# A new order of four engines' instructions in a batch loop of attention, head mixing and experts

## The reference, cut to what matters

```python
y = clip(((x * style0) @ W0.T) * demod0 + b0)          # per sample
Q, K, V = y@Wq, y@Wk, y@Wv                             # 16 heads in 4 groups, 64 wide
A = softmax(Q K^T / 8) V                               # over 128 keys
x = x + y + A @ Wpost
kx = modulated_linear(x)                               # q = k = v = kx
# per token: 16 heads of 8 features attend to one another
A2 = softmax(einsum('bnhd,bnjd->bnhj', kx, kx) / sqrt(8))
t = modulated_linear(einsum('bnhj,bnjd->bnhd', A2, kx))
x = x + experts(t)                                     # top 2 of 8 experts, capacity 640
```

## Time and profile before

| | |
|---|---|
| median of 3 runs | 538.81 us (537.04 to 538.97) |
| profiled execution | 537.42 us, its span 535.5 us |
| busy share of the span | PE 94%, PEld 67%, DVE 78%, ACT 70%, POOL 60% |
| granted TensorE clock | full in all 40 slices of the page |
| transfers | 7.19 MB in all, at the start and at the end |

### The profile page before, as it was taken

One profiled execution on the slowest core, in us unless ns is written; L12 is line 12 of the kernel. 1 busy time (PEld: TensorE's weight loads), 2 busy tenths in 40 slices (PEclk: granted clock), 3 DMA queues, 4 the chain that ended last, 5 costly groups with the idle time before them and its releaser, 6 DMA issues.

```text
span 535.5 us, 12870 instructions
## 1 busy us (share of the span) xinstructions
PE 504.0 (94%) x3896; PEld 356.4 (67%) x3896; DVE 419.3 (78%) x715; ACT 372.5 (70%) x851; POOL 323.4 (60%) x328
## 2 busy tenths in 40 slices
PE   7899999999999999999999999999999979969997
PEld 7766666666666666666666666666666756656665
DVE  4234788888888888888888888888888877754766
ACT  3467777777777777777777777777777537657783
POOL 1103677777777777777777777777777657203860
PEclk9999999999999999999999999999999999999999
DMA  6500000000000000000000000000000000000004
GB/s 228 135 1 2 2 1 2 1 0 0 0 0 0 0 0 0 0 0 0 0 0 0 0 0 0 0 0 0 0 0 1 1 2 0 2 0 2 0 11 148
DMA packets 9364, 7.19 MB, mean 13 GB/s; under 512 B 1088, under 2 KB 8832, under 8 KB 9216
## 3 DMA queue, kind: packets, MB, share of 16 engines
q1 hardware_dynamic: 9344, 6.94, 4.3%
HBM read 4.84 MB, written 2.10 MB: 13 GB/s over the span
## 4 chain that ended last, share of the span: by engine, by line
PE 52%; issue 16%; ACT 13%; DVE 12%; POOL 2%; ACTq 1%; DMA 1%; SPq 1%; DVEq 0%; POOLq 0%
PE misc L704 6%; PE bank_a L697 6%; PE bank_t L679 5%; PE bank_d L712 5%; PE bank_t L947 4%; PE bank_s L664 4%; ACT prob L1001 4%; PE bank_d L689 4%; DVE mix_lo L447 3%; DVE attT L308 3%; PE bank_t L674 2%; PE bank_s L955 2%; PE bank_d L955 2%; DVE h_den L437 2%; PE misc L834 2%
## 5 line engine op out<-in xcount | busy, mean ns | idle before, releaser
L1362 POOL TENSOR_TENSOR pair<-kx 128x1152 f32<-128x1152 f32 x32 | 82.7, 2584 | 115.2 <-DVE shifted L418 93.2
L300 DVE TENSOR_REDUCE row_max<-bank_s 128x4 bf16<-128x512 f32 x128 | 89.3, 697 | 43.0 <-PE bank_s L664 38.1
L1347 POOL TENSOR_TENSOR mix_hi<-mix_hi 128x512 f32<-128x512 f32 (+2 forms) x96 | 104.8, 1092 | 7.5
L712 PE MATMUL bank_d<-attT,wpost_sb 128*128 128x128 f32 x512 | 70.7, 282 | 1.6 <-DVE attT L308 0.6
L1001 ACT ACTIVATE prob<-bank_t 128x512 f32<-128x512 f32 x128 | 68.8, 593 | 3.6 <-PE bank_t L679 3.6
L704 PE MATMUL misc<-yT,wq_sb 128*128 128x128 f32 x512 | 68.2, 277 | 0.0
L712 PEld LDWEIGHTS bank_d<-attT,wpost_sb 128*128 128x128 f32 x512 | 62.0, 192 | 7.0 <-DVE attT L308 6.8
L679 PE MATMUL bank_t<-qT,kT 64*128 64x256 f32 x512 | 65.7, 376 | 0.0
L308 DVE TENSOR_TENSOR attT<-bank_a,inv_den 128x512 f32<-128x512 f32 x64 | 43.8, 686 | 25.1 <-ACT inv_den L1001 14.4
L704 PEld LDWEIGHTS misc<-yT,wq_sb 128*128 128x128 f32 x512 | 62.9, 194 | 0.7
L1340 POOL TENSOR_TENSOR mix_hi<-weight,kx 128x1024 f32<-128x1024 f32 x32 | 63.0, 1970 | 0.0
(11 more groups left out here) (183 smaller groups left out, 943.7 us busy)
## 6 DMA issues: line engine op xcount, KB each, us to landing
out<-acc_all SPq DMA_DIRECT2D x8, 256.0 KB, 2.3
x_all<-in_xT SPq DMA_DIRECT2D x1, 1024.0 KB, 9.8
w_sb<-in_w SPq DMA_DIRECT2D x2, 512.0 KB
x_all<-in_xT SPq DMA_DIRECT2D x1, 768.0 KB, 7.5
wq_sb<-in_wq SPq DMA_DIRECT2D x1, 512.0 KB, 6.1
wpost_sb<-in_wpost SPq DMA_DIRECT2D x1, 512.0 KB, 9.7
x_all<-in_xT SPq DMA_DIRECT2D x1, 256.0 KB, 3.2
b_rows<-in_b SPq DMA_DIRECT2D x16, 4.0 KB
```

Of the source, the lines that this page charges most:

```text
L300: V.tensor_reduce(bass.AP(row_max, first_w * (P + 1) + HPG * p, [[HPG * P, P], [P + 1, 2], [KEY, 2], [1, 1]]), bank_s[:, :, :].rearrange(" ...
L712: last = mm(bank_d[:, 0, :], wpost_sb[:, k, :], attT[:, k, :], start=(k == 0), stop=(k == CHUNKS - 1))
L1347: G.tensor_tensor(mix_hi[:, jd, 0:r, :], mix_hi[:, jd, 0:r, :], mix_hi[:, jd, r:2 * r, :], ALU.add).then_inc(s_hi, 1)
L1362: G.tensor_tensor(pair[:, :, :], bass.AP(kx2, jc * 2 * P, [[4 * P, P], [0, SHIFTS], [1, P]]), bass.AP(kx2, jc * 2 * P, [[4 * P, P], [MD, S ...
```

## The change

Within a step of the loop the helpers are called in another order on all four engines; nothing is added or removed from a step. On TensorE the fourth strip's scores come before the first half of the queries, tokens_made comes behind the first transposed scores, the y product before keys_turned and the second strip's scores, and the third strip's scores and mixing_turned stand between the halves of attend. On VectorE the sum mix_sum, the maximum h_max and shifted become separate calls, and the maxima of strips two and three move. On ScalarE six evacuations change places. On GpSimd the product for mix_hi comes first in the step, and the last two halvings behind the mirrored scores. Three fillers more stand in the first step.

```diff
@@ VectorE, loop_slot
                     if D:
                         weight_sums()
+                        weight_inverses()
                         weighted_rows()
                     if C:
                         attended()
                     head_scores()
                     if D:
                         row_sum()
+                    head_maxima()
                     if A:
                         heads_max(a, 0)
+                        heads_max(a, 1)
                     if D:
-                        weight_inverses()
-                    mixed(mix_part[:, :])
+                        rows_joined()
+                    head_shift()
+                    mixed()
                     if A:
-                        heads_max(a, 1)
-                    head_shift()
+                        heads_max(a, 2)
                     if has(a + 1):
...
                     if B:
                         normalise(s, 0)
-                    if A:
-                        heads_max(a, 2)
@@ TensorE, loop_slot
+                    if B:
+                        scores(s, j, 3)
                     if A:
                         pe.wait_ge(s_yT, n(a))
                         queries(a, 0)
-                    if B:
-                        scores(s, j, 3)
-                    if has(d - 1):
-                        tokens_made(d - 1)
...
                     if B:
                         scores_t(s, j, 0)
+                    if has(d - 1):
+                        tokens_made(d - 1)
...
                         denominators(s)
                         attend(s, j, 0)
-                        if C:
-                            pe.wait_ge(s_kx2, n(c))
-                        attend(s, j, 1)
+                    if A:
+                        scores(a, ja, 2)
                     if D:
                         if A:
                             pe.wait_ge(s_q, 2 * n(a))
                         mixing_turned(d)
-                    if A:
-                        scores(a, ja, 2)
+                    if B:
+                        if C:
+                            pe.wait_ge(s_kx2, n(c))
+                        attend(s, j, 1)
@@ ScalarE, slot
                 if A:
                     copy_q(a, ja, 0)
-                    narrow_q(a, ja, 0)
                 if B:
...
                     f(neg_diag[:, j, :, :], bank_s[:, :, :], scale=-1.0).then_inc(s_neg, 1)
-                if has(d - 1):
-                    tokens_out(d - 1)
+                if A:
+                    narrow_q(a, ja, 0)
                 if C:
                     x1_scaled()
                 if B:
                     exp_scores(s, 0)
                     exp_scores(s, 1)
+                if has(d - 1):
+                    tokens_out(d - 1)
...
+                head_weights()
                 if B:
                     invert_den(s)
-                head_weights()
```

More of the change, by code:

```diff
@@ L390, in slot, with rows_joined, mixed @@
                 ja, jc, jh, jd = 1 - j, 1 - j, j, 1 - j
-                def mixed(low):
+                def rows_joined():
+                    dve.wait_ge(s_lo, 4 * d + 4)
+                    dve.wait_ge(s_hi, 4 * d + 4)
+                    V.tensor_tensor(mix_sum[:, :], mix_part[:, :], mix_hi[:, jd, 0, :], ALU.add).then_inc(s_msum, 1)
+                def mixed():
                     if D:
-                        dve.wait_ge(s_lo, 4 * d + 4)
-                        dve.wait_ge(s_hi, 4 * d + 4)
-                        V.tensor_tensor(mix_sum[:, :], low, mix_hi[:, jd, 0, :], ALU.add).then_inc(s_msum, 1)
                         dve.wait_ge(s_hrden, n(d))
@@ L856, in loop_slot @@
                         gate_logits(parts_early[3])
+                    if has(a + 1):
+                        if A:
+                            pe.wait_ge(s_v, n(a))
+                        pe.wait_ge(s_xs, n(a + 1))
+                        mm(misc[0][:, 0, :], modw_sb[:, 0, :], xs[:, j, :], start=True, stop=True).then_inc(s_y_mm, 1)
                     if C:
@@ L861, in loop_slot @@
                     if s_is(s, -1):
-                        keep_going(3)
-                    if has(a + 1):
-                        if A:
-                            pe.wait_ge(s_v, n(a))
-                        pe.wait_ge(s_xs, n(a + 1))
-                        mm(misc[0][:, 0, :], modw_sb[:, 0, :], xs[:, j, :], start=True, stop=True).then_inc(s_y_mm, 1)
+                        keep_going(6)
                     if B:
@@ L1194, in slot @@
                         f(k16[rows, ja, :, half, :], misc[0][rows, 0:2, :]).then_inc(s_k16, 1)
-                if C:
-                    keys_out()
-                if A:
+                    need(act, s_t_mm, 4 * n(a - 2))
+                    f(kT[:, ja, :, :], misc[0][:, 0:2, :]).then_inc(s_k, 1)
                     need(act, s_av_mm, 2 * n(a - 2))
@@ L1200, in slot @@
                       misc[0][:, 2:4, :].rearrange("p a (g e) -> p (a g) e", e=KEY)).then_inc(s_v, 1)
+                if C:
+                    keys_out()
                 if B:
@@ L1207, in slot @@
                     keys_twice()
+                if A:
+                    narrow_q(a, ja, 1)
                 if has(a + 1):
@@ L1330, in slot, with halved @@
                     pool.wait_ge(s_ld_x, 32)
-                if A:
-                    pool.wait_ge(s_yT, n(a))
-                if has(s + 2):
-                    xs_of(s + 2, j)
-                if A:
-                    G.tensor_tensor(x_all[:, col(a)], x_all[:, col(a)], yT[:, :], ALU.add).then_inc(s_xy, 1)
+                def halved(i, r):
+                    pool.wait_ge(s_hi, 4 * d + i + 1)
+                    G.tensor_tensor(mix_hi[:, jd, 0:r, :], mix_hi[:, jd, 0:r, :], mix_hi[:, jd, r:2 * r, :],
+                                    ALU.add).then_inc(s_hi, 1)
                 if D:
@@ L1344, in slot @@
                                     ALU.mult).then_inc(s_hi, 1)
-                    for i, r in enumerate((4, 2, 1)):
-                        pool.wait_ge(s_hi, 4 * d + i + 1)
-                        G.tensor_tensor(mix_hi[:, jd, 0:r, :], mix_hi[:, jd, 0:r, :], mix_hi[:, jd, r:2 * r, :],
-                                        ALU.add).then_inc(s_hi, 1)
+                if A:
+                    pool.wait_ge(s_yT, n(a))
+                if has(s + 2):
+                    xs_of(s + 2, j)
+                if A:
+                    G.tensor_tensor(x_all[:, col(a)], x_all[:, col(a)], yT[:, :], ALU.add).then_inc(s_xy, 1)
+                if D:
+                    halved(0, 4)
                 if H and (not isinstance(s, int) or s < BATCH):
```

18 lines of the change are left out of this document (9 added, 9 removed).

## The result

The changed kernel takes 519.03 us (median of 4 runs, 517.53 to 519.11), the kernel before 537.92 in the runs beside it (4 runs, 536.99 to 538.97): ratio 0.9642, 95% interval 0.962 to 0.9664. The gain is 18.9 us, the forecast was 14.8 (538.8 to 524.0).

The account below looks back on a forecast made before the run. TensorE, busy 94%, was taken as the bound: per step 0.83 us of waiting gone, 0.27 added, 12.86 to 12.30, taken as 12.32; 28 steps give 15.1, net 14.8, so 524.0 us from 538.8. Range 520 to 538.

Parts of the forecast that it names:

- the pair of borders: TensorE, between attend's halves: two more array-shape changes per step would add 0.27 us, bounds 0.09 to 0.49.
- the early steps: First steps without mixing: a 0.31 us stop traded for 0.27 us of shape changes, counted as no gain.
- the last step: Last step of the loop: the second half of attend comes later, adding 0.3 us.
- The stop before the second pair of transposed scores: TensorE waits there for the exponentials, held up through mix_lo, x_all and x1s; 0.52 us per step would go.
- The stop before the post products: TensorE, before the second half of the post products: 0.31 us per step would go, fourth strip's scores coming earlier.
- part 5: Third strip's scores and turned mix between attend's halves: two more array-shape changes, costing 0.27 us per step.
- The base: Profiled time forecast at 522.6 us, raised 1.4 because the median shown lay above the profiled run: 524.0.
- the bounds that I had worked out myself: Added array-shape changes around attend's split: 0.09 us if only entry costs, up to 0.49 us per step.
- ScalarE's part, cost nothing: ScalarE's reordered evacuations: costed at nothing; at most one swapped instruction of 0.4 to 0.6 us on the exponentials.
- The loop through VectorE: Second bound: fourth maximum through first maximum, TensorE's products and VectorE again, 12.1 us, 0.2 below TensorE's 12.32.
- GpSimd keeps the access through xs, x_all or the halving: mix_lo delayed 0.4, 0.8 or 2.0 us: smaller gain (chance 0.15), no change (0.08), slower, 575 us (0.14).
- The milder slower case: Array-shape changes costing 0.45 with half the stops left: step 12.9 us or more; slower outcomes together had chance 0.14.

Follow-up runs that it names:

- e1: Kernel before the change with only GpSimd's queue in the new order: 524.77 us, ratio 0.979 to the kernel before.
- e2: Changed kernel with GpSimd's queue back in the old order: 532.91 us, ratio 0.9937 to the kernel before.
- e8: Kernel before with GpSimd's new order, and the third strip's scores and turned mix between attend's halves: 530.0 us, ratio 0.9854.
- e4: Changed kernel with ScalarE's queue back in the old order: 544.59 us, ratio 1.0138 to the kernel before.
- e3: Changed kernel with attend's halves together again, the third strip's scores and the turned mix behind them: 539.01 us, ratio 1.0025.
- e7: Changed kernel with the fourth strip's scores again behind the first half of the queries: 538.46 us, ratio 1.0012.
- e5: Changed kernel with the tokens product moved between the first transposed scores' two kinds of products, two array-shape changes more per step: 532.6 us, ratio 0.9901.
- e6: Changed kernel with VectorE's reciprocal moved back behind the mixing rows and row maxima: 518.33 us, ratio 0.9629.

## Where the prediction held, and the steps of its sum that failed

The mechanism held. Two terms of the step's sum failed: the pair of borders was taken at 0.27 and cost 0.19, and a wait of 0.10 before the fourth scores was not in the sum at all. Beside them, the early steps were put at nothing and gave 1.05.

Of the profiled time 18.4 us went (537.42 to 519.01), 18.5 of them span. By the timelines, before against after: 0.69 before the first transposed scores, 1.05 in the first three steps, 27 x 0.657 = 17.7 in the full steps, less 0.53 in the last step and 0.47 behind it.

- **The stop before the second pair of transposed scores** (0.52): gone, 0.51 in the step shown, 0.49 in the mean of the 27. The chain of causes holds at each link: mix_lo 1.93 to 1.35, x1s's wait 1.72 to 0.51, no idle for prob; e1 does it alone, e2 brings it back.
- **The stop before the post products** (0.31): gone; it gave 0.25 in the mean, with 1.51 to 1.27 for the two rows together. The second half still takes 1.04 to the next row, of which 0.98 was expected.
- **A wait that the sum did not have**: 0.10. The first query half took from 0.95 to 1.04 to the fourth strip's scores behind it, 0.99 in the mean, since these waited for the third maximum; now nothing of that kind stands there (0.89). The prediction put TensorE's waiting at 0.83 from two places and left this one at nothing. In 27 steps 2.7 us.
- **The pair of borders** (0.27, part 5): the term that was mis-sized. From the row sums to the product behind attend, the turned mix and the third scores are 3.28 us (274.69 to 277.97) and were 3.10 (275.09 to 278.19), 0.18 more, 0.19 in the mean. No run has this pair alone; e8 bears it out only together with its query product. I had added 0.07 for a float32 weight load behind the second border. But the turned mix had paid that load already behind whole attend, and the product behind the border is now a bf16 one. The 0.08 come to 2.2 us. In means the step is 0.49 + 0.25 + 0.10 - 0.19 = 0.65, of 0.657 measured; the prediction had 0.52 + 0.31 - 0.27 = 0.56 and took 0.54.
- **The early steps** ("nothing") gave 1.05. There the stop before the second post half was the larger one: from the negation at 49.26 to the post products at 49.85 in the kernel before, 48.27 to 48.49 after. A row of a full step stood for them. Measured for the last step -0.53 for an expected -0.3.
- **The base**: I added 1.4 because the median shown, 538.81, lay above the profiled 537.42. The four runs beside the change have a median of 537.92, and the changed kernel's median equals its profiled time. Of the 5.0 us between 524.0 and 519.03 this is 1.4; the step is 2.6, the early steps 1.05, the start 0.69, and the end -0.7. The 1.4 and the 0.69 are spread and say nothing about the mechanism; without them the time would be 521.1, inside the range. The step and the early steps are errors of the working.

The range failed at its lower end: it was put 1 us under a step of 12.2, while the bounds that I had worked out myself (0.09 for the borders) allowed 12.12.

**ScalarE's part, cost nothing**: right, but by e4 only together with TensorE's part. **The loop through VectorE** (12.1, 0.2 below TensorE): in the changed trace it is 7.87 (266.18 to 273.35 + 0.70), 2.92 and 1.43, of which about 0.28 is slack before the second strip's scores: 11.94, 0.28 below. It binds in e2 alone, where the second strip's scores start 0.05 behind the end of the first maximum. In e3 and e7, where one maximum comes late, 0.32 and 0.2 still lie between the two, and the loss is a stop of TensorE on a short path behind one strip's scores.

**The rivals.** That GpSimd keeps the access through xs, x_all or the halving is excluded by three traces: in e1 mix_lo arrives during xs and goes before x_all, in e3 during x_all and before the halving, in the change during the product and before xs. The Trainium skill (SBUF — State Buffer, Who interferes with whom) describes the lock and says that the order of issue decides who blocks; of a hand-over to an instruction that already waits it says nothing more. The traces agree with the order of issue: mix_lo was issued 0.32, 0.17 and 0.23 before the GpSimd instruction that then waited. So "VectorE goes first" and "the one issued first goes first" can't be told apart here, since in no trace did a waiting GpSimd instruction stand there before mix_lo was issued. The milder slower case, borders at 0.45 with half of the stops left, had a true part: e5 measures 0.4 for a pair and 0.1 for a wait that came with it, but for borders with 64 rows and float32 products behind them, which the change does not add. The Trainium skill (TensorEngine Tiling (Array Packing), Key Properties) says that a change of the tiling mode drains the array; the runs agree, with about 0.1 per border, and a weight load left uncovered behind it costs as much again.

**The parts are not additive.** GpSimd's order alone gives 0.47 per step, the other parts 0.19 more (12.404 to 12.217). Yet undoing GpSimd's part, the third strip's place, ScalarE's part or the fourth strip's place costs 0.58, 0.68, 0.97 and 0.61. With GpSimd's order kept, e3, e4 and e7 (12.82 to 13.19) are slower than e1, which has none of the other three engines' changes (12.404); the split of attend alone costs 0.18 on top of e1. So those orders fit each other, and undoing one of these moves is worse than having none of the three engines' changes. The 0.19 was measured for the set only; what each of its parts would give alone is not known but for the split of attend.

## What to carry to other kernels

- Where long elementwise products on VectorE and GpSimd hold each other up, look at which one the critical chain waits for, and let it be issued shortly before the other engine's product ends: here the waiting instruction then went first, and the wait fell on what came behind on the other engine. One engine's order gave two thirds of this gain.
- Price a change of the array's shape together with the product that stands first behind it, and read that price at each border; put a bf16 product there.
- For a stop read off one step, check the same place in several full steps and in the first ones: one wait went by turns between 0.06 and 0.15, and the first steps had another stop than the full ones.
- When a run hits the expected time, look in its trace for the waits that the expectation named. e3 and e7 hit it with the named loop still slack.

## What the hardware showed that I had not expected

- A VectorE product that was issued while a GpSimd instruction ran got the access before GpSimd's next instruction each time: xs took 1.38 us for 0.40, x_all 1.44 for 0.45, a halving 2.27 for 1.27.
- One pair of borders between 128 and 32 columns costs 0.19 us with a bf16 product first behind it (the changed kernel) and 0.29 with a float32 one (e8), one between 64 and 128 rows with float32 products behind the borders 0.40 (e5).
- A wait that the profile names before a weight load behind a border need not be one: 0.84 stands before that load in the changed kernel, in e7 and in e8, with three different releasers.
- An instruction that waits for this access can be issued up to 0.4 us earlier and end at the same time (e6).
